# Four edits to a two-layer attention and expert kernel: paired output weights, squares over 128 rows, the null column first, eight expert buffers

## The reference

```python
xn = ln(x, g_norm)
q  = (xn @ Wq).reshape(b, n, 16, 64).transpose(0, 2, 1, 3)
k, v = split(xn @ Wkv)                    # one key and one value head for all 16 query heads
k = concat([null_k, k]); v = concat([null_v, v])
q = l2norm(q) * q_scale; k = l2norm(k) * k_scale      # layer 0 only
sim = q @ k.T * scale + concat([null_bias, bias])
sim = where(mask & causal, sim, -max)
out = softmax(sim) @ v                    # 16 heads of 64 = 1024 columns
out = ln(out @ Wout, g_out)               # the output projection, 1024 -> 256
...
# layer 0: x = x + spikes(square(relu(out @ W_fc.T)) @ W_proj.T)
# layer 1: x = x + block(out): a small attention, then for each token a shared expert
#          and the two best of eight experts, silu(x W1) * (x W3) @ W2, weighted and added
```

## Time and profile before

| | us |
|---|---|
| median of 3 runs | 1536.22 |
| lowest, highest | 1531.81, 1537.91 |
| the profiled execution | 1532.06 |
| its span | 1530.3 |
| PE, DVE, ACT, POOL busy | 1341.0, 1130.7, 884.1, 810.9 |
| mean granted TensorE clock | 0.954 of full |

### The profile page before, as it was taken

The page is one execution under the profiler, slowest core; times in us unless marked ns, Lnnn a source line. Parts: engine busy times, 40 slices in busy tenths (PEclk is TensorE's granted clock), DMA queues, the critical chain, the costliest instruction groups (busy, mean ns, idle before and its releaser), DMA issues.

```text
span 1530.3 us, 43531 instructions
## 1 busy us (share of the span) xinstructions
PE 1341.0 (88%) x15534; PEld 1170.8 (77%) x15535; DVE 1130.7 (74%) x2217; ACT 884.1 (58%) x2209; POOL 810.9 (53%) x844
## 2 busy tenths in 40 slices
PE   1799999999669999989999999668997199999994
PEld 0689889898559999878888888557886178888883
DVE  4498888888834645789999998568883996445457
ACT  1566676766536666646656665347774165445544
POOL 1356665665414545465555554278873206777713
PEclk9999999999979999999999999979997599999997
DMA  7200000000130000000000000010002222232354
GB/s 203 42 28 9 8 9 9 8 9 8 32 82 1 1 0 0 1 10 9 7 9 9 9 8 13 19 50 15 14 15 90 89 87 74 96 96 97 92 183 157
DMA packets 89683, 65.04 MB, mean 42 GB/s; under 512 B 50862, under 2 KB 84401, under 8 KB 89522
## 3 DMA queue, kind: packets, MB, share of 16 engines
q1 hardware_dynamic: 82610, 44.98, 10.7%
q0 software_dynamic: 6912, 17.84, 3.7%
HBM read 39.18 MB, written 18.35 MB: 38 GB/s over the span
## 4 chain that ended last, share of the span: by engine, by line
PE 75%; DVE 11%; issue 5%; ACT 5%; POOL 1%; SPq 1%; DMA 0%; DVEq 0%; ACTq 0%; POOLq 0%
PE psW L1898 12%; PE psQ L1819 12%; PE psQ L2179 8%; PE psW L2161 5%; PE psS L1880 4%; PE psS L1923 4%; PE psT L1856 3%; PE psQ L1992 3%; PE psW L1980 3%; PE psM L1980 3%; PE psS L1992 3%; PE psM L1867 2%; PE psM L2153 2%; PE psT L2169 1%; PE psM L1837 1%
## 5 line engine op out<-in xcount | busy, mean ns | idle before, releaser
L712 POOL TENSOR_TENSOR pn<-ex,rden 128x1024 f32<-128x1024 f32 x64 | 144.6, 2259 | 244.1 <-PE psT L1856 239.5
L1819 PEld LDWEIGHTS psQ<-xT,wq 128*128 128x128 f32 x1536 | 196.6, 196 | 46.0 <-issue 24.1
L1898 PE MATMUL psW<-wout,oT 128*128 128x256 f32 x1536 | 210.2, 292 | 16.5 <-ACT oT L945 14.4
L1819 PE MATMUL psQ<-xT,wq 128*128 128x256 f32 x1536 | 216.5, 293 | 1.5 <-ACT cur L1026 1.5
L1898 PEld LDWEIGHTS psW<-wout,oT 128*128 128x128 f32 x1536 | 195.3, 194 | 29.3 <-ACT oT L945 24.0
L2179 PE MATMUL psQ<-W,exT 128*128 (+1 forms) x624 | 172.5, 412 | 0.1
L757 POOL TENSOR_TENSOR hT<-hf,hT 128x512 fp32r<-128x512 f32 x64 | 84.5, 1321 | 99.7 <-ACT hT L1022 99.7
L2179 PEld LDWEIGHTS psQ<-W,exT 128*128 128x128 f32 x624 | 110.9, 191 | 19.4 <-issue 0.4
L830 POOL DMA_INDIRECT rows<-xf,src x72 | 72.3, 1005 | 72.5 <-issue 57.3
L1322 DVE SCALAR_TENSOR_TENSOR oT<-psS,nvcol,oT 128x512 fp32r<-128x512 f32 x128 | 89.7, 740 | 24.0 <-ACT oT L945 23.5
L2161 PE MATMUL psW<-W,ehT 128*128 (+1 forms) x624 | 100.7, 297 | 5.7 <-DVE ehT L1758 5.7
(11 more groups left out here) (299 smaller groups left out, 3479.7 us busy)
## 6 DMA issues: line engine op xcount, KB each, us to landing
both<-results SPq DMA_DIRECT2D x16, 512.0 KB, 8.3
raw_w<-W SPq DMA_DIRECT2D x27, 256.0 KB, 4.8
vv<-vp SPq DMA_DIRECT2D x256, 16.0 KB, 1.8
xf<-xf_all SPq DMA_DIRECT2D x4, 1024.0 KB
out<-X SPq DMA_DIRECT2D x8, 512.0 KB, 2.9
X<-x SPq DMA_DIRECT2D x1, 3584.0 KB, 15.2
raw_q<-Wq SPq DMA_DIRECT2D x2, 1024.0 KB, 5.9
bvv<-v_all SPq DMA_DIRECT2D x128, 16.0 KB, 1.8
```

What stands on the lines that cost most here:

```text
L712: nc.gpsimd.tensor_tensor(pn[:], ex[t % 2][:, :, 0:S], rden[:].unsqueeze(2).to_broadcast([P, H, S]), ALU.mult).then_inc(sem("t_pn"), 1)
L1819: mm = nc.tensor.matmul(psQ[:, cc, h * QT:h * QT + QT], wq[w][:, k, c * P:c * P + P], xT[g % 2][u][:, k, :], start=(k == 0 and j == 0), st ...
L1898: mm = nc.tensor.matmul(psW[:, 0:D], oT[u][:, c, :], wout[w][:, c, :], start=(u == 0 and c == 0 and w == 0), stop=(u == 1 and c == CH - 1))
```

## The change

The diff makes four independent edits and some renaming of semaphores.

1. **Output projection.** `wout` becomes one tile with the high and low weights of a chunk side by side. PE takes the high part of oT once against 512 columns (both), 8 calls, then the low part against 256 columns, 8 calls. psW then holds two partial sums. ACT copies the second half to O, and DVE adds the first half to it in a new instruction at the end of its step; only then is psW free.
2. **Squares.** 8 calls of 128 rows, 128 tokens and both columns of `ind`, in place of 32. All results lie in psM, so ACT copies them in one instruction in place of two. The wait of the squares for psW goes.
3. **Null column** of layer 1 ahead of the scores, as in layer 0.
4. **Experts.** 8 buffers in place of 4. 32 steps are written out ahead of the loop, which has 7 turns of 8 steps. 12 fetches stand ahead of the first store, and the fetch of tile r+12 behind the store of tile r. `by_end` moves to another place, and SP waits for it before it loads the last experts.

```diff
+BUFS = 8
...
-    for i in range(0, FIRST + 8):
-        step(i, i % 4)
+    for i in range(0, FIRST + 2 * BUFS):
+        step(i, i % BUFS)
...
-    with eng.Fori((FIRST + 8) // 4, end // 4) as quad:
-        for m in range(4):
-            step(4 * quad + m, m, "routed")
+    with eng.Fori((FIRST + 2 * BUFS) // BUFS, end // BUFS) as turn:
+        for m in range(BUFS):
+            step(BUFS * turn + m, m, "routed")
...
-        wout = [sb("attw", f"wout{i}", [P, CH, D], F32R) for i in range(2)]
+        wout = sb("attw", "wout", [P, CH, 2, D], F32R)
...
-        SS = 512 - G2 * CH
+        SS = 512 - G2 * H
...
-        rows = sb("tile", "rows", [P, 4, D], F32)
+        rows = sb("tile", "rows", [P, BUFS, D], F32)
...
+            sp.wait_ge(sem("r_given"), 2)
...
+            ahead = BUFS + 4
+            for r in range(ahead):
+                fetch(r, r % BUFS)
...
-                            for half, bank in enumerate((psM, psW)):
-                                ins = nc.scalar.activation(qss[:].rearrange("p j (c a) -> p j c a", a=2)[:, :, :, half],
-                                                           bank[:, SS:512].rearrange("p (j c) -> p j c", c=CH), ACT.Copy)
-                            ins.then_inc(sem("t_ssev"), 1)
+                            nc.scalar.activation(qss[:].rearrange("p j h -> p (j h)"), psM[:, SS:512], ACT.Copy).then_inc(sem("t_ssev"), 1)
...
-                        nc.scalar.activation(O[:, t, :], psW[:, 0:D], ACT.Copy).then_inc(sem("t_oev"), 1)
+                        nc.scalar.activation(O[:, t, :], psW[:, D:2 * D], ACT.Copy).then_inc(sem("t_olow"), 1)
...
+                            nc.vector.tensor_tensor(e[:, :, S], sn[t % SN][:], nbias[:], ALU.add).then_inc(sem("t_null"), 1)
                             dve.wait_ge(sem("t_bm"), t + 1)
                             nc.vector.tensor_tensor(by_slot(e[:, :, 0:S]), scores, by_slot(masked[:]), ALU.add).then_inc(sem("t_left"), 1)
-                            nc.vector.tensor_tensor(e[:, :, S], sn[t % SN][:], nbias[:], ALU.add).then_inc(sem("t_null"), 1)
...
+                    t = i - LATE
+                    if live(t):
+                        dve.wait_ge(sem("t_olow"), done + t + 1)
+                        nc.vector.tensor_tensor(O[:, t, :], psW[:, 0:D], O[:, t, :], ALU.add).then_inc(sem("t_oev"), 1)
...
-                    reach(pe, sem("t_oev"), i - LATE)
                     for cc in range(2):
                         for h in range(2):
                             for j in range(G2):
-                                for half in range(2):
-                                    for b in range(2):
-                                        at = SS + j * CH + 2 * (n + cc) + h
-                                        f = slice(half * DH, half * DH + DH)
-                                        mm = nc.tensor.matmul((psM, psW)[half][b * S:b * S + S, at:at + 1],
-                                                              sqT[cc][f, h, j * P + b * S:j * P + b * S + S], ind[f, half:half + 1],
-                                                              start=True, stop=True, skip_group_check=True)
+                                at = SS + j * H + 2 * (2 * (n + cc) + h)
+                                mm = nc.tensor.matmul(psM[:, at:at + 2], sqT[cc][:, h, j * P:j * P + P], ind[:],
+                                                      start=True, stop=True, skip_group_check=True)
...
+                            n = 2 - u
                             for c in range(CH):
-                                for w in range(2 - u):
-                                    mm = nc.tensor.matmul(psW[:, 0:D], oT[u][:, c, :], wout[w][:, c, :],
-                                                          start=(u == 0 and c == 0 and w == 0), stop=(u == 1 and c == CH - 1))
+                                mm = nc.tensor.matmul(psW[:, 0:n * D], oT[u][:, c, :], wout[:, c, 0:n, :].rearrange("p n d -> p (n d)"),
+                                                      start=(u == 0 and c == 0), stop=(c == CH - 1), skip_group_check=True)
...
-                    if m == 0:
+                    if m % 4 == 0:
```

More of the change, by code:

```diff
@@ L54 @@
 NOWHERE = 1 << 20
+BUFS = 8
 EW = 3 * KD * D
+REL = dict(ln=1, act=2, Tp=3, T=4, mm=5, out=6)
 WHOLE = 1.5 * 2.0 ** 23
@@ L827, in fetch @@
                 apart(pool, (sem("e_src"), r + 1))
-                if not isinstance(r, int) or r > 3:
-                    apart(pool, (sem("e_xTp"), FIRST + r - 3))
+                if not isinstance(r, int) or r >= BUFS:
+                    apart(pool, (sem("e_xTp"), FIRST + r - BUFS + 1))
                 nc.gpsimd.indirect_dma_start(out=rows[:, m, :], out_offset=None, in_=xf_dram,
@@ L845, in _ @@
             pool.wait_ge(sem("xf_stored"), 16 * 5)
-            for r in range(8):
-                fetch(r, r % 4)
-            with pool.Fori(0, ROUTED // 4 - 2) as quad:
-                for m in range(4):
-                    store_result(4 * quad + m, m)
-                    fetch(4 * quad + m + 8, m)
-            for r in range(ROUTED - 8, ROUTED):
-                store_result(r, r % 4)
+            ahead = BUFS + 4
+            for r in range(ahead):
+                fetch(r, r % BUFS)
+            turns = (ROUTED - ahead) // BUFS
+            with pool.Fori(0, turns) as turn:
+                for m in range(BUFS):
+                    store_result(BUFS * turn + m, m)
+                    fetch(BUFS * turn + m + ahead, (m + ahead) % BUFS)
+            for r in range(BUFS * turns, ROUTED):
+                store_result(r, r % BUFS)
+                if r + ahead < ROUTED:
+                    fetch(r + ahead, (r + ahead) % BUFS)
             for g in range(len(SUM_STEP)):
@@ L2146, in expert_step @@
                     if kind(t, shared) == "routed":
-                        pe.wait_ge(sem(f"e_rows{m}"), loaded(t - FIRST, m))
-                        tile = rows[:, m, :]
+                        n = (m - FIRST) % BUFS
+                        pe.wait_ge(sem(f"e_rows{n}"), loaded(t - FIRST, n))
+                        tile = rows[:, n, :]
                     else:
```

95 lines of the change are left out of this document (49 added, 46 removed).

## The result

The changed kernel takes 1570.84 us (median of 4 runs, 1569.31 to 1575.6) beside 1535.43 us for the kernel before on the same chip: ratio 1.0238, interval 1.0219 to 1.0257, so 35.4 us slower. A later set gave 1.0234 (1.0217 to 1.0252). I had predicted 1547.6 us, 1533 to 1559: the direction was right, the size a third of what came. The profiled execution took 1571.61 us, its span is 1569.9 us, 39.6 more than that of before.

A forecast was written before the change was run, and what follows sets the result against it. PE was taken to bound layer 0 and the experts, with layer 1 staying at 10.20 us. The terms 18.6 - 2.5 + 0.9 + 0 - 5.6 = +11.4 us, on the median of 1536.22, gave 1547.6 us, range 1533 to 1559.

The forecast's parts named there:

- Part 1: Squares of layer 0: 16 whole-array loads cost 0.69 us more per step, 27 steps, +18.6 us (bounds -21 and +28).
- Part 2: Output projection in layer 0: pairing the weights wins 0.08 us per tile, 32 tiles, -2.5 us (bounds -1.6 and -4).
- Part 3: New DVE addition, 0.41 us: free in layer 0 while the bias addition leads pn by 0.48 us; +0.9 us in all.
- +0.9 for two ends: At the end of each layer the addition stands alone behind the last tile: 2 x 0.45 us.
- Part 4: Null column of layer 1 moved ahead of pn: DVE still waits behind POOL, the period stays 10.20 us, 0 us.
- second rival: Layer 1: DVE gets ahead of POOL's L721 and PE sets the pace, -6.6 us, 1541 us; chance 0.12.
- Part 5: Experts: loop turns go from 16 to 7 at 0.62 us each, -5.6 us.
- first rival: Layer 0: the order of bias addition and pn turns over, 0.8 to 0.9 us per step, +26 us, 1573 us; chance 0.11.

The follow-up runs named there:

- squares only: The kernel before with only the squares of layer 0 changed, over all 128 rows in 8 calls per step: 1566.02 us, ratio 1.0197.
- the pair alone: The kernel before with only the paired output projection and the new DVE addition, squares on quarters, half their sums unread: 1553.46 us, ratio 1.0118.

## Why the prediction was wrong, step by step

- **Part 1, squares, +18.6.** This is the term that failed most: alone it measured +29.7. The price of a load was right: 0.111 us beside 0.109. Three things were not. First, the sum set 1.75 us against 1.06, 0.69 more; from load to load it is 1.70 against 1.06, 0.64 more, but around them two stretches grew that it left out. From the start of the scores' loads, which take quarters of the array, to the squares' first load it is 1.24 us after and 1.09 before, and from the key's load to that of pT 0.14 after and 0.06 before. The three make 0.87, beside 0.85 measured (squares only), 22 us over 26 steps. That the change from quarter to whole array is the reason of the 0.15 is argued, not shown. Second, "the first five lie before about 94 us, where the chain doesn't stand on PE" was the failed assumption: in a fill the chain passes through PE for the squares too, +4.6 us, of which 2.3 go with the clock. Third, a fall of the clock in 0 to 2 steps, 1.5 us each.
- **Part 2, projection, -2.5.** The loads of its 16 matmuls take 2.90 us where those of 24 took 2.94; by the steps 0.035 to 0.065 us per tile, -1 to -2 us. Right within its bounds in the second case.
- **Part 3, addition.** Its length (0.36 to 0.43 us) and the order of bias addition and pn held, with a lead of 0.70 us where I had 0.48. That the margin was thin is shown by the pair alone, where the order turns. "+0.9 for two ends" failed: the five last steps of layer 0 take 55.5 to 57.9 us in the six rows of the table with the addition and 51.9 to 53.5 in those without, +4.0 by their means. The sum had priced the addition behind the last tile alone. In the changed kernel the step that ends at 443.25 takes 14.41 us, where its like before took 10.67:

```profile
429.26 0.42 DVE L1342 TENSOR_TENSOR O<-psW,O 128x256 f32<-128x256 f32 x1 [0.63 <-ACT O L967]
429.60 2.28 DVE L1423 TENSOR_TENSOR wpr<-raw_pr,wpr 128x2048 fp32r<-128x2048 f32 x1
431.80 1.88 DVE L1283 TENSOR_TENSOR ex<-sn,rq 128x16 f32<-128x16 f32 x1
...
431.36 2.29 POOL L716 TENSOR_TENSOR pn<-ex,rden 128x1024 f32<-128x1024 f32 x1 [2.58 <-PE psT L1862]
...
435.18 1.86 PE L1886 MATMUL psS<-pT,vv 64*64 64x512 f32 x8 [3.97 <-DVE ex L1286]
438.46 4.76 PE L1904 MATMUL psW<-wout,oT 128*128 128x512 f32 x16 [1.42 <-ACT oT L950]
```

and before:

```profile
397.83 2.23 DVE L1413 TENSOR_TENSOR wpr<-raw_pr,wpr 128x2048 fp32r<-128x2048 f32 x1
399.97 0.17 DVE L1277 TENSOR_TENSOR ex<-sn,rq 128x16 f32<-128x16 f32 x1
...
400.30 1.90 POOL L712 TENSOR_TENSOR pn<-ex,rden 128x1024 f32<-128x1024 f32 x1 [2.25 <-PE psT L1856]
...
401.63 1.09 PE L1880 MATMUL psS<-pT,vv 64*64 64x512 f32 x8 [1.48 <-DVE ex L1280]
404.16 2.17 PE L1898 MATMUL psW<-wout,oT 128*128 128x256 f32 x16 [1.44 <-ACT oT L945]
407.21 1.21 PE L1898 MATMUL psW<-wout,oT 128*128 128x256 f32 x8 [0.88 <-DVE oT L1322]
```

The addition waits for ACT's copy (0.63 us), and behind it stands the preparation of wpr, the next stage's weights. The null column L1283 behind that now comes after pn's start and is locked out for 1.88 us, where before it was through in 0.17, and with the squares only in 0.18: the lock that the sum had weighed for the bias addition in a steady step. PE idles 5.39 us (3.97 and 1.42) in place of 3.80. Its two products then run at 1.2 GHz, 435.4 to 442.2, and take 6.62 us in place of 4.47. The two differences, 1.6 and 2.15, are the step's 3.74. The kernel before has such a fall one step later, with 4.80 us for the same projection, so the fall itself isn't new; but over the five last steps PE is at 1.2 GHz for 17 us after and for 10 before. Before the first tile of layer 1 the rows with the addition have 246.4 to 246.9 us and those without 245.0 to 246.2, where the column is in its old place: some 1 us by the means, and hardly clear of the scatter.
- **Part 4, null column, 0.** Right for the steady steps: 10.20 us, the column at 0.19 us, the subtraction still behind POOL's masked bias. Failed for the rest: I looked at the steady step alone. In the fill of layer 1 it costs 3.5 us, in its last steps 2.9, the larger part of each for the column locked out by pn and the rest for PE at 1.2 GHz behind it. The second rival (DVE gets ahead of POOL, 0.14 us per step) needs the addition to be absent; then it is exactly that, 10.06.
- **Part 5, experts, -5.6.** Mis-sized: the chain's stops after are 21.2 us apart (1393.72 to 1414.90), eight steps of 2.54 are 20.3, so this turn of eight costs 0.86 us, not 0.62; four turns of the chain cost 0.72 to 0.90, 0.81 on average. 7 x 0.81 = 5.7, or 6.0 by the turn shown, against 16 x 0.62 = 9.9: -3.9 to -4.2; -3.9 by the two profiles and -3.5 by the medians of the part alone. Why a turn of eight costs more isn't shown.

```profile
1393.72 0.38 issue
...
1414.90 0.48 issue
```

The sum as the stages have it, by means of the rows with a part and without it: fill 4.6, steady layer 0 +21, its end 4.0, start of layer 1 4.8, its end 3.5, experts -3.9: +34, beside +35.4 measured. Of the 24 us I missed, 16 lie in the fills and ends of the two layers (the 0.9 I had there taken off), 5 in the steady steps of layer 0 and 2 in the experts. That the first rival's 1573 us lies within 3 us of the measured time is luck: its turned order isn't in the steady steps of the changed kernel.

## What to carry to other kernels

Price an edit in the fill and the drain of a pipeline too: there the chain passes through every engine, and work that a steady step hides, or that meets no lock there, stands in it in full. Fewer instructions aren't cheaper where the old ones ran on quarters of the array side by side: 64 loads took 1.06 us up to the next line's load, 16 whole ones 1.70. Where two engines exclude each other, compute the lead of the one over the other for each variant; here 0.4 us decided 0.6 us per two steps in layer 0 and 0.14 per step in layer 1.

## What the runs showed of the hardware that I had not expected

- The granted clock fell to 0.50 while the trace has PE busy without a gap, in a row of 32 loads of 128 x 128 f32 with two moving columns each; it cost 3.2 us of a 17.0 us step, in one trace. As many loads in two rows of 16 kept it at 0.99. Whether it is the loads or the near absence of streaming isn't told apart by these runs. The Trainium skill ("TensorE: Matmul & The Clock Gate", HAM oscillation) puts such falls down to idle gaps of PE; by that rule this one would not come, and the trace disagrees, with PE busy for 1.60 of 1.60 us where the clock fell.
- A lock between DVE and POOL restored itself: the step that lost the order delayed the next pn, so that steps alternate (11.15 and 11.75 us).
- In one set the experts' part took some 55 us longer in all kernels on a chip that showed none of it in the next set. Its cause is open.
